# Edge counts of a graph layer, transposed by DMA through DRAM in place of TensorE transposes and ScalarE copies (one Trainium2 core)

## The reference

```python
h = jnp.maximum(_layernorm(x), 0.0)
# layer 0
s = jax.nn.sigmoid(h @ wenc.T + benc)                 # 1250 x 500
msgs = (s @ conv_weight)[src] * edge_weight[:, None]
agg = jax.ops.segment_sum(msgs, dst, num_segments=1250)
x = x + (agg + s @ lin_weight.T) @ wdec.T + bdec
# layer 1
h = jnp.maximum(_layernorm(x), 0.0)
row, col = edges with a self loop added for every node   # row = src, col = dst
h = h @ W.T + b
deg = zeros.at[row].add(1.0)
norm = deg[row] ** -0.5 * deg[col] ** -0.5
x = x + jax.ops.segment_sum(norm[:, None] * h[col], row)
```

## Time and profile before

| what | value |
|---|---|
| median of 3 runs | 483.14 us (483.09 to 483.29) |
| the profiled execution | 483.09 us |
| its span in the trace | 481.3 us |
| TensorE busy | 472.9 us, 98% of the span |
| VectorE, ScalarE, GpSimd busy | 59%, 45%, 23% |
| the chain that ended last, share of TensorE | 94% |
| granted TensorE clock | 1.0 of full speed |
| moved by DMA | 38.39 MB |

### The profile page before, as it was taken

One profiled execution on the slowest core, in us unless ns is written; L12 is line 12 of the kernel. 1 busy time (PEld: TensorE's weight loads), 2 busy tenths in 40 slices (PEclk: granted clock), 3 DMA queues, 4 the chain that ended last, 5 costly groups with the idle time before them and its releaser, 6 DMA issues.

```text
span 481.3 us, 8778 instructions
## 1 busy us (share of the span) xinstructions
PE 472.9 (98%) x3907; PEld 422.0 (88%) x3407; DVE 285.9 (59%) x545; ACT 215.9 (45%) x433; POOL 110.6 (23%) x106
## 2 busy tenths in 40 slices
PE   7999999999999999999999999999999999999996
PEld 5899999988899999999977778999999887777775
DVE  7898887896439279030457888795311085344443
ACT  6998986664438204162504455513324422321210
POOL 3300000000050000000003333100004399895640
PEclk9999999999999999999999999999999999999999
DMA  8620004000000150000091000553320133613113
GB/s 320 234 89 2 1 2 170 4 1 1 2 2 0 23 201 7 1 2 1 31 398 51 1 0 2 203 221 132 132 94 1 43 131 130 226 70 86 43 45 88
DMA packets 11887, 38.39 MB, mean 80 GB/s; under 512 B 2480, under 2 KB 2541, under 8 KB 11203
## 3 DMA queue, kind: packets, MB, share of 16 engines
q1 hardware_dynamic: 11619, 37.39, 21.2%
q0 software_dynamic: 224, 0.39, 0.3%
HBM read 27.53 MB, written 10.24 MB: 78 GB/s over the span
## 4 chain that ended last, share of the span: by engine, by line
PE 94%; DVE 2%; ACT 2%; issue 1%; POOL 0%; POOLq 0%; DVEq 0%
PE ps L1369 89%; PE ps L1373 3%; PE ps L1389 1%; ACT junk L654 1%; PE ps L1611 1%; PE ps L1610 1%; DVE welo L971 1%; ACT zhi L683 0%; ACT wide L659 0%; DVE thr_half L908 0%; ACT wehi L670 0%; DVE x1b L1359 0%; ACT xn L676 0%; PE ps L1618 0%; PE ps L1519 0%
## 5 line engine op out<-in xcount | busy, mean ns | idle before, releaser
L1369 PE MATMUL ps<-C,ghi 125*128 125x250 f16 x400 | 85.5, 270 | 0.0
L1369 PE MATMUL ps<-C,glo 125*128 125x250 f16 x400 | 85.5, 269 | 0.0
L1359 DVE SCALAR_TENSOR_TENSOR x1b<-ps,dsc,x1b 125x512 f32<-125x512 f32 x50 | 35.9, 747 | 36.2 <-PE ps L1369 36.0
L1369 PE MATMUL ps<-Ahi,h2hi 125*125 125x250 f32 x200 | 56.4, 282 | 0.0
L1369 PE MATMUL ps<-Alo,h2hi 125*125 125x250 f32 x200 | 55.8, 279 | 0.0
L1369 PE MATMUL ps<-Ahi,h2lo 125*125 125x250 f32 x200 | 55.8, 279 | 0.0
L598 POOL TENSOR_TENSOR glo<-t,ghi 125x512 f16<-125x512 f32 x18 | 20.6, 1165 | 143.3 <-ACT t L844 143.3
L610 POOL TENSOR_TENSOR S<-U 128x500 f32<-128x500 f32 x25 | 31.6, 1273 | 84.6 <-DVE Blo L1333 60.0
L1369 PEld LDWEIGHTS ps<-C,ghi 125*128 125x128 f16 x400 | 38.7, 97 | 4.3 <-issue 0.3
L1369 PEld LDWEIGHTS ps<-C,glo 125*128 125x128 f16 x400 | 39.0, 97 | 3.7
L1369 PE MATMUL ps<-zhi,wehi 128*125 128x250 f32 x160 | 40.6, 290 | 0.6 <-ACT zhi L683 0.6
(11 more groups left out here) (185 smaller groups left out, 1145.8 us busy)
## 6 DMA issues: line engine op xcount, KB each, us to landing
xn<-in_x_dram SPq DMA_DIRECT2D x10, 512.0 KB, 7.4
x<-in_x_dram SPq DMA_DIRECT2D x10, 512.0 KB
x_scratch<-x SPq DMA_DIRECT2D x10, 500.0 KB
x1b<-x_scratch SPq DMA_DIRECT2D x10, 500.0 KB
out_dram<-x1b SPq DMA_DIRECT2D x20, 240.0 KB
B<-in_W_dram SPq DMA_DIRECT2D x4, 1024.0 KB, 8.1
wd<-in_wdec_dram SPq DMA_DIRECT2D x1, 2048.0 KB, 8.5
we<-in_wenc_dram SPq DMA_DIRECT2D x4, 500.0 KB, 6.2
```

The source lines that it names most:

```text
L1359: v.scalar_tensor_tensor(r, ps[bank8["w", u, m]][0:PB, 0:512], scale, r, ALU.mult, ALU.add).then_inc(*term_ok.up(u, m, n))
L1369: return t.matmul(o_ap, lhsT, rhs, start=start, stop=stop)
```

## The change

The counts are written to DRAM and read back transposed. SP writes the ten blocks of `C` to a new scratch tensor `c_scratch` (1265 rows of 1250 float16) as soon as each has its self loops, and one more piece that fills the rows behind 1250. After the loads of `x1` and `bb` it issues ten transposing DMAs. The d-th reads 1264 rows of 128 numbers (256 bytes, 2500 bytes apart), and writes them as 128 partitions of 1264 numbers to `CT[:, d, :]`. `CT` is a tile of its own name; it lies over the place of `C` and the last 240 bytes of the fifth `A`, which are no longer needed by then. TensorE takes `CT` in place of `C` and waits once, after decode, for the last of the ten. The transposes on TensorE, the copies on ScalarE, their two signals and their waits are gone.

```diff
+NT = 1264
...
+    CT = at("CT", RH - NB * 2 * NT, [128, NB, NT], F16)
...
+    c_d = nc.dram_tensor("c_scratch", (NT + 1, N), F16)
...
     def sync(q):
...
+        for k in range(NB):
+            q.wait_ge(*diagC.at(k))
+            q.dma_start(c_d.ap()[k * PB:(k + 1) * PB, :], C[0:PB, k, :]).then_inc(*d_c.up(k))
+        q.dma_start(c_d.ap()[N:NT + 1, :], C[0:NT + 1 - N, 0, :]).then_inc(*d_c.up(NB))
         q.wait_ge(*dinv_ok.at())
         q.dma_start(dinv_d[0].rearrange("(k p) -> p k", p=PB), col["dinv"][0:PB, :],
...
         for k in range(NB):
             q.dma_start(x1[:, k, :], x[k]).then_inc(*d_x1[k].up("x"))
         q.dma_start(bb[0:PB, :], b.to_broadcast([PB, DIM])).then_inc(*d_bb.up())
+        q.wait_ge(*va_ok.at(NB - 1))
+        q.wait_ge(*d_c.at(NB))
+        for d in range(NB):
+            q.dma_start(CT[:, d, :], bass.AP(tensor=c_d, offset=d * PB, ap=[[N, NT], [1, 128]]), transpose=True
+                        ).then_inc(*d_ct.up(d))
...
     def scalar(a):
...
-                for n, (k, js) in enumerate(turns.get((g, fo), ())):
-                    turn_put(g, fo, n, k, js)
...
-        for half in range(2):
-            a.wait_ge(*turned.at("d", half))
-            for i in range(5):
-                k = 5 * half + i
-                ins = a.activation(C[0:PB, k, k * PB:(k + 1) * PB],
-                                   ps[6 + half][0:PB, :].bitcast(F16)[:, i * 128:i * 128 + PB], ACT.Copy)
...
     def tensor(t):
...
-                        for i, j in enumerate(js):
-                            t.transpose(view[:, i * 128:i * 128 + PB], C[0:PB, k, j * PB:(j + 1) * PB], identh[0:PB, 0:PB])
-                            ins = t.transpose(view[:, (m + i) * 128:(m + i) * 128 + PB], C[0:PB, j, k * PB:(k + 1) * PB],
-                                              identh[0:PB, 0:PB])
...
-            o_ap, ct = bank[:, 0:GN], C[0:PB, d, u * GN:(u + 1) * GN]
+            o_ap, ct = bank[:, 0:GN], CT[0:PB, d, u * GN:(u + 1) * GN]
...
             decode()
-            t.wait_ge(*ct_ok.at("d", 1))
+            t.wait_ge(*d_ct.at(NB - 1))
             u_and_w(extra)
```

More of the change, by code:

```diff
@@ L170, in build @@
     C = at("C", RC, [128, NB, N], F16)
+    CT = at("CT", RH - NB * 2 * NT, [128, NB, NT], F16)
+    assert RFREE + 2 * 2528 <= RH - NB * 2 * NT
     h32 = [at(f"h32_{g}", RH + g * H_SLOT, [128, FB, GN], F32) for g in range(NG)]
@@ L296, in windows_of @@
         return range(i * BATCH, min(NWIN, (i + 1) * BATCH))
[L298 to L307, removed]
     SEQ = [("u", u, k) for u in range(NG) for k in range(KB)] + [("w", u, m) for u in range(NG) for m in ORDER]
@@ L339, in build @@
     d_wd = signal("d_wd", [()], 16)
+    d_c = signal("d_c", one(NB + 1), 16)
+    d_ct = signal("d_ct", one(NB), 16)
     d_x1 = [signal(f"d_x1_{k}", [("x",), ("away",), ("biased",)], 16) for k in range(NB)]
@@ L405, in build @@
     va_ok = signal("va_ok", one(NB))
-    turn_keys = [(g, fo, n) for (g, fo), t in turns.items() for n in range(len(t))] + [("d", 0), ("d", 1)]
-    turned = signal("turned", turn_keys)
-    ct_ok = signal("ct_ok", turn_keys)
     wdhi_ok = signal("wdhi_ok", one(FB))
@@ L795, in degree @@
                          ).then_inc(*deg_a.up(k))
[L797 to L804, removed]
         split_A(0, 0)
@@ L824, in scalar @@
                 a.activation(col["sq"][0:PB, :], col["dr"][0:PB, :], ACT.Sqrt).then_inc(*sq_ok.up())
-        for half in range(2):
-            a.wait_ge(*turned.at("d", half))
-            for i in range(5):
-                k = 5 * half + i
-                ins = a.activation(C[0:PB, k, k * PB:(k + 1) * PB],
-                                   ps[6 + half][0:PB, :].bitcast(F16)[:, i * 128:i * 128 + PB], ACT.Copy)
-            ins.then_inc(*ct_ok.up("d", half))
         def norm2_root(k):
@@ L1589, in agg_edges @@
             ins.then_inc(*agg_done.up(g, fo))
[L1591 to L1596, removed]
         def aggregate():
@@ L1603, in aggregate @@
                     agg_edges(g, fo)
[L1604 to L1608, removed]
-                        for i, j in enumerate(js):
-                            t.transpose(view[:, i * 128:i * 128 + PB], C[0:PB, k, j * PB:(j + 1) * PB], identh[0:PB, 0:PB])
-                            ins = t.transpose(view[:, (m + i) * 128:(m + i) * 128 + PB], C[0:PB, j, k * PB:(k + 1) * PB],
-                                              identh[0:PB, 0:PB])
-                        ins.then_inc(*turned.up(g, fo, n))
-            for half in range(2):
-                view = bank_of_turn(("d", half), half)
-                for i in range(5):
-                    k = 5 * half + i
-                    ins = t.transpose(view[:, i * 128:i * 128 + PB], C[0:PB, k, k * PB:(k + 1) * PB], identh[0:PB, 0:PB])
-                ins.then_inc(*turned.up("d", half))
         def degrees_extra():
@@ L1655, in bank_of @@
             if b4 is None:
-                t.wait_ge(*(ct_ok.at("d", bank - 6) if bank >= 6 else x1_ok.at(*KC[18 + bank if bank < 2 else 12 + bank])))
+                if bank < 6:
+                    t.wait_ge(*x1_ok.at(*KC[18 + bank if bank < 2 else 12 + bank]))
             else:
@@ L1741, in tensor @@
             second_half(False)
-        for done in (agg_done, turned, dec_done, u_done, w_done):
+        for done in (agg_done, dec_done, u_done, w_done):
             done.n = 0
```

1 line of the change is left out of this document (removed).

## The result

The changed kernel takes **484.95 us** (median of 8 runs, 483.87 to 485.10) where the kernel before takes 483.14: a ratio of 1.0031 [1.0022, 1.0040]. It is 0.3% slower, and the prediction said 1.1% faster. The runs of this kernel lie further apart than those of before, and TensorE's mean granted clock is lower in them (0.991 to 0.996 of full speed, where that of before is 0.998 to 1.0). The clock doesn't account for the whole spread: two runs at 0.996 took 483.87 and 484.14, a third 485.05.

What follows compares the result with a forecast made beforehand. TensorE was taken to bound the kernel, holding 94% of the chain of waits. 6.07 us for transposes less 0.4 for `wdlo` and 0.2 for late `dinv_row` left 5.5 off 483.1: 477.6 us, range 477.0 to 493.

Steps and rivals of the forecast that it cites:

- The transposes' 6.07 us: TensorE, groups 2 to 4 of aggregation up to decode: removing all 100 transposes saves 6.07 us, covered by nothing.
- ScalarE's copies, worth nothing: ScalarE in aggregation: removing its copies of transposed blocks gains nothing, since it waited 55.3 us for TensorE there.
- The wait for `wdlo`, 0.4: Start of decode: without the diagonal transposes as cover, TensorE waits 0.4 us for the last part of `wdlo`.
- The writes' length, 24.8 us: Ten writes of `C` on five DMA engines, ahead of `dinv`: 24.8 us, ending at 159.7.
- What is queued behind them: Write of `dinv` and `dinv_row` come 1.5 us late; with 1.33 slack at group 2's last `agg_lin`, TensorE loses 0.2 us.
- the whole gain is gone at 30 us of writes: Writes of `C` ahead of `dinv`: if they take 24.8 + 5.5 = 30 us, nothing of the gain is left.
- worst case: Writes of `C` at 0.154 us a packet take 38.5 us, end at 173.4 and cost TensorE 13 us.
- The reads, 0 us: Ten transposing reads before the u stage: 17 us, hidden in some 41 us, so 0 us cost.
- Rival 1: Transposed counts come late ahead of the u stage: 492.6 us on five engines, 481 or 517 one by one; chance 0.25.
- Rival 3: TensorE's saved time returns as a wait for `ghi` or `glo` at the u stage: 483 us; chance 0.05.
- Rival 2: Writes of `C` hold up `dinv`: 479 to 483 us for 26 to 30 us, 490.4 at 38.5; chance 0.09.

Runs made afterwards that it cites:

- run 2: Changed kernel with each write of `C` cut into 120 rows and 5, still ahead of `dinv`: 477.41 us, ratio 0.9881.
- Run 9: Kernel of run 2 with `wdhi` and `wdlo` made earlier, two parts behind each of pieces (4,0) and (4,1): 476.83 us, ratio 0.9869.
- run 7: Changed kernel with SP waiting for `dinv_row` before it issues the load of the decoder's weight: 482.66 us, ratio 0.9992.
- run 4: Kernel before, transposes kept, with the eleven writes of `C` added ahead of `dinv` and read by nobody: 486.57 us, ratio 1.0073.
- run 6: Kernel of run 2 with extra VectorE sums behind `dinv_row`: five 486.70 us, three 482.70; five plus 36 more TensorE matmuls ahead of the wait 484.93.
- run 3: Changed kernel with 36 more matmuls on TensorE ahead of its wait in group 2: 481.59 us, ratio 0.9968.
- run 8: Kernel of runs 1 with fifteen more transposing reads ahead of the ten that count: 488.94 us, ratio 1.0119.
- runs 1: Changed kernel with the eleven writes of `C` moved behind the issue of `dinv_row` on SP: 477.37 us, ratio 0.9879.

## Why the prediction was wrong

**The transposes' 6.07 us: right.** 58.77 and 58.92 for 64.99 (run 2 and the count of the earlier trace rows). The gain of the change in kind was where the prediction put it.

**ScalarE's copies, worth nothing: right.** Ahead of `hhi` ScalarE stands idle 68.1 us for TensorE in the profile's page of the changed kernel, so it has time to spare without the copies too, and groups 2 to 4 gained no more than the transposes.

**The wait for `wdlo`, 0.4: right in kind, 0.5 in size.** Run 9 removed it, and it gave 0.58 between the medians.

**The writes' length, 24.8 us: nearly right.** They began when reckoned and ended at 161.8, so 26.8 us, 0.106 for a packet of 2500 bytes where the line gave 0.099. SP was free at 150.6 (reckoned 150). This is 2.0 of the trouble.

**"What is queued behind them", 1.5 us late: the step that failed.** Measured 5.9. It is made of four parts: the 1.5 as reckoned, 2.0 of longer writes, 1.0 more until the write of `dinv` was reported done (SP waited 11.1 us for it, 6.5 before; the difference of 4.6 is these three parts together), and 1.35 more for `dinv_row` on its way back, of which run 7 gives 0.7 to the decoder's weight. The rest of that is no more than rows differ by from trace to trace (table in run 4). The working moved the start of one transfer and left everything behind it as long as before; yet both transfers of the chain were longer too. With a slack of 1.33, which was right, the 1.5 became 0.2 and the 5.9 became 4.6. A term with a slack in it is not proportional to its error: 4.4 us more of lateness were 4.4 us more of wait. The text even had the warning, that the whole gain is gone at 30 us of writes, but reckoned only with the writes' own length. (Its worst case has a slip: writes that end at 173.4 and not at 158.2 are 15.2 late and not 14.5, which makes 491 of the 490.4 and stays within the range.)

**The clock: a term that was missing.** A wait of 4.6 us cost 6.3 to 7.1, by the length of groups 2 to 4 in the two profiles of the changed kernel and in run 2 (65.04 and 65.90 for 58.77). No wait of TensorE in this stretch of the trace of before was long enough to show it, and the prediction priced idle time at its own length. The effect is shown by making the idleness without a DMA and by filling it again (run 6); run 3 agrees but doesn't show it alone. Without this term the wait would have left a gain of about 1 us, 482 for 483.1; the wait takes most of the gain and the clock makes a loss of it.

**The reads, 0 us: right, for a price somewhat off.** From the end of the loads of `x1` until the last `CT` they ran some 22 us (reckoned 17), which is about 148 GB/s for their 3.24 MB. Windows at the time and at their end in the changed kernel:

```profile
260.00:270.00 10.00, 10.00 (x45) 8.00 (x44) 7.51 (x23) 5.51 (x8) 3.32 (x3) 1.00 1.13 179
275.00:280.00 5.00, 5.00 (x24) 3.97 (x23) 4.17 (x13) 1.81 (x3) 1.54 (x2) 1.00 0.03 7
```

All ten are there by 275.3, and TensorE wants them at 295.98: 20 us to spare. By an estimate from the Trainium skill's price of 1309 ns for one block ("VectorE: DVE Perf Modes", section "The three transpose paths") the 99 blocks would have taken 129 us one after another; the stream takes 0.22 us for each, so the measurement decides against it here. The Trainium skill's other page, "Advanced Engine Details and Errata", section "X-Bar Transpose (TRN2)", has them as fast as regular transfers; these ran at some 150 GB/s where the loads of `x1` ran at 404 just ahead of them, so that isn't borne out either.

**The rivals.** Rival 1, with a chance of 0.25, didn't occur; it takes 25 reads to bring it about (run 8). Rival 3, a pace set by `ghi` and `glo`, didn't either: runs 1, 2 and 9 keep the whole gain. Rival 2, with a chance of 0.09, was the right one, by the wait it named and the sign it gave by ("VectorE waiting for `dinv_row` past 176"): 177.61. Its condition, writes of 26 to 30 us, was met at 26.8; but it counted the writes' overhang alone, which gives 477.6 + 2.0 = 479.6 there, and 484.9 came. It deserved far more than 0.09: a slack of 1.3 us behind a chain of two landings of some 7 us each. That 484.95 lies between 477.0 and 493 is luck: the upper end was set that far for late counts and longer writes, and the time came there by longer landings and the clock, which the prediction doesn't have.

## What to carry to other kernels

A long write ahead of a small transfer that someone waits for can cost more than its overhang, as here, where both landings of the chain behind it were longer too; put it behind, or cut it so that more engines take it (120 + 5 rows instead of 125 made it 2.3 times as fast), and hold the sum against the slack at the waiting engine. Price a wait of TensorE of some microseconds at more than its length, and look at the granted clock behind it. A transposing read is worth having in place of TensorE's transposes when there is time to hide it: here the reads took 22 us, and there were 41 between the loads ahead of them and the first use.

## What the runs showed of the hardware

- TensorE's clock. Behind waits of 3.25, 3.69, 4.45, 4.57, 6.28 and 9.42 us the profiles show the half level (1.2 GHz), behind 2.69 and 2.85 they show the full one (2.4 GHz); but executions of one program differ (run 6: three sums, once at 1.0 and otherwise at 0.992 to 0.996 in the mean). The half level began while TensorE stood idle and lasted some 3 to 6 us beyond the first matmul behind the wait; in the profiled executions it cost 1.6 to 3.0 us. This wasn't expected in the prediction at all.
- The transposing reads of 1264 rows of 256 bytes take 2.0 to 2.2 us each in a stream, rounds or not, and one took a median of 4.8 us from issue to landing. SP is taken up by their issues for 1.7 to 2.8 us each. The share of the DMA engines reads above 1 while they run (1.13 from 260 to 270, 2.43 from 254 to 256), so it is no share any more there.
- Writes of 2500 bytes a row from 125 partitions run at 118 to 123 GB/s; cut into 120 and 5 partitions, at 279.
